# One-hot tables of a graph: wide one-hots and four sums per group, against factored one-hots and one sum

## The reference, cut to what matters

```
attn = ex / denom[src]                                    # softmax over the edges of each src, 4 layers
out = jax.ops.segment_sum(attn[:, :, None] * v[dst], src, num_segments=N)
...
msgs = x[col] * vals[:, None]                             # row = src, col = dst, vals = edge_weight
agg = jax.ops.segment_sum(msgs, row, num_segments=n)
return jnp.einsum('nd,od->no', agg, weight)
```

## Time and profile before

| | |
|---|---|
| time of the kernel, median of 3 runs | 1857.2 us (1856.85 to 1858.12) |
| the profiled execution's own time | 1858.3 us |
| its span in the trace | 1856.5 us |
| loop over the 56 groups, first matmul to last sum | 17.5 to 178.6 us |
| `tables_done` | 179.2 us |

### The profile page before, as it was taken

One profiled execution on the slowest core, in us unless ns is written; L12 is line 12 of the kernel. 1 busy time (PEld: TensorE's weight loads), 2 busy tenths in 40 slices (PEclk: granted clock), 3 DMA queues, 4 the chain that ended last, 5 costly groups with the idle time before them and its releaser, 6 DMA issues.

```text
span 1856.5 us, 30729 instructions
## 1 busy us (share of the span) xinstructions
PE 1746.2 (94%) x11805; PEld 1499.0 (81%) x11805; DVE 1240.5 (67%) x2366; ACT 904.8 (49%) x1468; POOL 432.2 (23%) x545
## 2 busy tenths in 40 slices
PE   4776999999999999999999999999999999999898
PEld 4665788888887888888888888887888888878777
DVE  7888865665866557658665665677557657675744
ACT  9996454554542445446433554554335446453221
POOL 3223230010282301001743010005621001036201
PEclk9898999999999999999999999999999999999899
DMA  3041552242310324224201332332104224240121
GB/s 126 2 131 49 215 174 89 95 129 89 109 44 22 100 78 145 95 75 131 65 26 54 113 122 82 109 115 76 35 30 130 89 80 149 84 152 30 42 88 65
DMA packets 63885, 168.62 MB, mean 91 GB/s; under 512 B 5957, under 2 KB 24250, under 8 KB 63735
## 3 DMA queue, kind: packets, MB, share of 16 engines
q10 hardware_dynamic: 23040, 102.41, 17.1%
q1 hardware_dynamic: 40700, 64.25, 10.8%
HBM read 145.04 MB, written 16.99 MB: 87 GB/s over the span
## 4 chain that ended last, share of the span: by engine, by line
PE 76%; DVE 12%; issue 5%; ACT 3%; DMA 1%; POOL 1%; DVEq 1%; SPq 0%; ACTq 0%; POOLq 0%
PE ps L1501 65%; PE ps L1724 9%; DVE prob L1254 2%; PE ps L1642 2%; DVE onehot L1061 1%; DVE CW L1094 1%; DVE PT_lo L1270 1%; DVE CW L1096 1%; DVE CW L1100 1%; ACT prob L853 1%; POOL x L663 1%; ACT PT_hi L871 1%; DVE CW L1092 1%; DMA piece<-in_L_gnn_m_w_dram 1%; DVEq L1084 1%
## 5 line engine op out<-in xcount | busy, mean ns | idle before, releaser
L871 ACT ACTIVATE PT_hi<-ps 128x512 fp32r<-128x512 f32 (+1 forms) x400 | 235.3, 588 | 244.8 <-PE ps L1724 244.6
L1270 DVE TENSOR_TENSOR PT_lo<-ps,PT_hi 128x512 fp32r<-128x512 f32 (+1 forms) x400 | 270.5, 677 | 50.9 <-ACT PT_hi L871 43.6
L853 ACT ACTIVATE prob<-prob,nmax 128x1250 f32<-128x1250 f32 x160 | 214.2, 1338 | 137.6 <-DVE nmax L1254 137.6
L1724 PE MATMUL ps<-ident,prob 128*128 128x128 f32 (+1 forms) x1600 | 245.3, 276 | 12.5 <-DVE PT_lo L1270 11.9
L1254 DVE CUSTOM_DVE_ANT_0 prob<-ps,Lr 128x1250 f32<-128x1250 f32 x160 | 232.3, 1452 | 32.0 <-PE ps L1501 30.7
L1724 PEld LDWEIGHTS ps<-ident,prob 128*128 128x128 f32 (+1 forms) x1600 | 179.5, 140 | 80.0 <-DVE PT_lo L1270 61.6
L1501 PE MATMUL ps<-PT_hi,v_hi 128*128 128x256 f32 (+1 forms) x800 | 226.7, 283 | 1.2 <-DVE PT_lo L1270 1.2
L1501 PE MATMUL ps<-PT_lo,v_hi 128*128 128x256 f32 (+1 forms) x800 | 225.0, 281 | 0.0
L1501 PE MATMUL ps<-PT_hi,v_lo 128*128 128x256 f32 (+1 forms) x800 | 224.3, 280 | 0.0
L1501 PE MATMUL ps<-yT,wqk_hi 128*128 128x512 f32 (+1 forms) x768 | 213.1, 364 | 0.0
L1501 PE MATMUL ps<-k_hi,q_hi 128*128 128x512 f32 (+2 forms) x480 | 191.9, 400 | 2.1 <-DVE k_lo L1233 2.1
(11 more groups left out here) (210 smaller groups left out, 3801.6 us busy)
## 6 DMA issues: line engine op xcount, KB each, us to landing
Lr<-l_table ACTq DMA_DIRECT2D x160, 625.0 KB, 3.9
piece<-in_L_gnn_m_w_dram SPq DMA_DIRECT2D x32, 256.0 KB, 2.8
w_table<-CW SPq DMA_DIRECT2D x5, 1250.0 KB, 8.0
prob<-w_table SPq DMA_DIRECT2D x10, 625.0 KB, 4.0
x<-in_x_dram SPq DMA_DIRECT2D x2, 2304.0 KB
CW<-CW SPq DMA_DIRECT2D x7, 625.0 KB
piece<-in_L_gnn_wo_dram SPq DMA_DIRECT2D x16, 256.0 KB, 4.8
piece<-in_L_gnn_wq_dram SPq DMA_DIRECT2D x15, 256.0 KB, 2.8
```

What stands on the lines that cost most here:

```text
L853: act.activation(buf, buf, ACT.Exp, bias=nmax[:, i % 4:i % 4 + 1], scale=-1.0, accum_out=prob[:, i % 3, N:N + 1]).then_inc(S["exped"], 1)
L871: act.activation(o, i, ACT.Copy).then_inc(S["pt_hi"], 1)
L1270: dve.tensor_tensor(lo, i, hi.bitcast(F32), ALU.subtract).then_inc(S["pt_split"], 1)
L1724: m = pe.transpose(bank(5 + n % 2, at * P, at * P + rows), prob[0:rows, (NT * h + 2 * g + j) % 3, d * P:(d + 1) * P], ident[0:rows, 0:rows])
```

## The change

A row s is now split into a tile and a rest, s = 128 t + r, and the product is factored the other way round. The left operand is the one-hot of r, 128 columns, as it is and multiplied by the three parts of the weight. The right operand is the one-hot of the place 28 t + (column in the window), 280 columns of fp8.

- VectorE writes the one-hots of r for the three blocks of a group in one compare (`rows`, 3 x 128 places), three groups ahead, behind the sum of the group.
- GpSimd multiplies them by the three parts in one instruction for each group (3 x 3 x 128 = 1152 places).
- ScalarE makes the one-hots of 280 places, three for each group.
- TensorE runs 12 matmuls of 280 columns (3 blocks x 4 parts); the three parts of the weight are summed in PSUM, so VectorE adds counts and weights in one instruction of 560 places.
- Ahead of the loop VectorE works out t, r and the place from the edges; two copies to `eT` that only the fallback needs move behind the first `rows`.
- The other work on VectorE is cut into smaller steps behind groups 4 to 9 (`angles`), 15, 16, 24, 25 (`row_rest`, halves) and 51 to 55 (`early_stats`, one tile each). `cond_rest` and `last_x` on GpSimd stand ahead of groups 36 and 46, and `first_hi` on ScalarE stands behind the loop.
- The loops are written out for all 56 groups, in one branch for each engine but TensorE.

The diff, cut to its core:

```diff
+PLACES = NT * WIN
 ...
-            onehot = sb("onehot", [P, SBUFS, 2, NP], BF16, prep)
-            oh8 = sb("oh8", [P, SBUFS, 2, NP], F8, prep)
+            left = sb("left", [P, SBUFS, GK, 4, P], BF16, prep)
+            right = sb("right", [P, SBUFS, GK, PLACES], F8, prep)
 ...  GpSimd
-            def weigh(c, lo, hi):
-                for part in range(3):
-                    ...
-                    m = pool.tensor_tensor(o, oh, wp.unsqueeze(3).to_broadcast([P, hi - lo, GK, WIN]), ALU.mult)
-                m.then_inc(e_parts, 1)
+            with pool.If(flag < 1):
+                for n in range(NG):
+                    for work in between.get(n, ()):
+                        work()
+                    pool.wait_ge(e_onehot, n + 1)
+                    factors = left[:, n % SBUFS]
+                    pool.tensor_tensor(factors[:, :, 1:4, :], factors[:, :, 0, :].unsqueeze(2).to_broadcast([P, GK, 3, P]),
+                                       wpart[:, :, n, :].rearrange("p k b -> p b k").unsqueeze(3).to_broadcast([P, GK, 3, P]),
+                                       ALU.mult).then_inc(e_parts, 1)
 ...  ScalarE
-                    for b in (2,) if n % CHUNK_G == BOTH else (1, 2):
-                        m = act.activation(oh8[:, n % SBUFS, b - 1, :], iota_h[:], ACT.Abs_reciprocal_sqrt, ...)
+                    for b in range(GK):
+                        m = act.activation(right[:, n % SBUFS, b, :], iota_h[:, 0:PLACES], ACT.Abs_reciprocal_sqrt, ...)
 ...  VectorE, ahead of the loop
+            dve.wait_ge(src_cast, 1)
+            link(dve.tensor_scalar(ef[:, 5, :], ef[:, 0, :], 1.0 / P, -(P - 1.0) / (2 * P), ALU.mult, ALU.add))
+            link(dve.tensor_scalar(ef[:, 5, :], ef[:, 5, :], MAGIC, None, ALU.add))
+            link(dve.tensor_scalar(ef[:, 5, :], ef[:, 5, :], -MAGIC, None, ALU.add))
+            dve.scalar_tensor_tensor(out=ef[:, 4, :], in0=ef[:, 5, :], scalar=-float(P), in1=ef[:, 0, :], ...).then_inc(rows_made, 1)
 ...
+            dve.scalar_tensor_tensor(out=ef[:, 5, :], in0=ef[:, 5, :], scalar=float(WIN), in1=ef[:, 1, :], ...).then_inc(off_made, 1)
 ...  VectorE, the loop
+            def rows(n):
+                dve.tensor_tensor(left[:, n % SBUFS, :, 0, :], iota_h[:, 0:P].unsqueeze(1).to_broadcast([P, GK, P]),
+                                  eT[:, 4, :, n].unsqueeze(2).to_broadcast([P, GK, P]), ALU.is_equal).then_inc(e_onehot, 1)
 ...
+            def group(n):
+                dve.wait_ge(e_sum, START + n + 1)
+                base = dve.value_load(grow_i[0:1, n:n + 1], min_val=0, max_val=N - WIN)
+                sums = ps[:, (n % 2) * 1024:(n % 2) * 1024 + 1024].rearrange("p (k s) -> p k s", k=2)[:, :, 0:PLACES]
+                both = CW[:, :, :, bass.ds(base, WIN)]
+                dve.wait_ge(e_chain, START + n)
+                dve.tensor_tensor(both, both, sums.rearrange("p k (t w) -> p k t w", w=WIN), ALU.add).then_inc(e_chain, 1)
+                if n + AHEAD < NG:
+                    rows(n + AHEAD)
 ...  TensorE
-                    for s in range(NT):
-                        for b in range(GK):
-                            ...
-                            m = mm(ps[:, at:at + 4 * WIN], oh8[...] if by_act else onehot[...], win[...], b == 0, b == GK - 1)
+                    for b in range(GK):
+                        for part in range(4):
+                            o = ps[:, at:at + PLACES] if part == 0 else ps[:, at + 512:at + 512 + PLACES]
+                            m = mm(o, left[:, n % SBUFS, b, part, :], right[:, n % SBUFS, b, :],
+                                   b == 0 and part < 2, b == GK - 1 and part in (0, 3))
```

More of the change, by code:

```diff
@@ L86 @@
 HALF = NP // 2
-BOTH = 0
 HOT = 2.0 ** -6
@@ L107 @@
 )
-assert NT == 10 and NG % UNROLL_G == 0 and UNROLL_G % SBUFS == 0
+assert NT == 10
 LBUFS = 4
@@ L612, in last_x @@
                 pool.memset(x[:, NT - 1, :], 0.0).then_inc(f_set, 1)
[L614 removed]
+            between = {36: (cond_rest,), 46: (last_x,)}
             pool.wait_ge(eplan, 2)
[L617 to L636 removed]
+            flag = pool.value_load(grow_i[0:1, NG:NG + 1], min_val=0, max_val=1)
+            linked = link_n[0]
+            with pool.If(flag < 1):
[7 more added lines that the diff above has]
+                                       ALU.mult).then_inc(e_parts, 1)
+            with pool.Else():
+                link_n[0] = linked
+                for n in sorted(between):
+                    for work in between[n]:
+                        work()
             pool.wait_ge(bias_copied, 1)
@@ L792, in _ @@
                        28: (cond_copy,), 31: (lambda: row_hi(2),), 39: (cond_stack,),
-                       **{44 + 2 * n: (lambda n=n: first_hi(n),) for n in range(AHEAD_PIECES)}}
+                       }
             act.wait_ge(eplan, 2)
@@ L809, in _ @@
                         work()
+            for n in range(AHEAD_PIECES):
+                first_hi(n)
             act.wait_ge(tables_done, 1)
@@ L1051, in _ @@
             dve.wait_ge(iota_cast, 1)
[L1053 to L1068, removed]
+            def rows(n):
+                dve.tensor_tensor(left[:, n % SBUFS, :, 0, :], iota_h[:, 0:P].unsqueeze(1).to_broadcast([P, GK, P]),
+                                  eT[:, 4, :, n].unsqueeze(2).to_broadcast([P, GK, P]), ALU.is_equal).then_inc(e_onehot, 1)
+            for n in range(AHEAD):
+                rows(n)
+            dve.wait_ge(edges_turned, 4)
+            turned(0, 4)
+            turned(2, 5)
             flag = dve.value_load(grow_i[0:1, NG:NG + 1], min_val=0, max_val=1)
@@ L1124, in row_rest @@
-            def row_rest(i):
+            def group(n):
[7 more added lines that the diff above has]
+                    rows(n + AHEAD)
@@ L1133, in _ @@
-            between = {1: (angles,), 2: (lambda: row_rest(0),), 3: (lambda: row_rest(1),), NG // UNROLL_G - 1: (early_stats,)}
-            for i in range(NG // UNROLL_G - 1):
-                for work in between.get(i, ()):
-                    work()
-                with dve.If(flag < 1):
-                    groups(i)
-            for work in between[NG // UNROLL_G - 1]:
-                work()
-            with dve.If(flag < 1):
-                groups(NG // UNROLL_G - 1)
-                dve.wait_ge(e_chain, START + 3 * NG)
-                dve.wait_ge(e_count, START + NG)
+                first_stats(t)
@@ new lines, in _ @@
+            between = {**{4 + n: (lambda n=n: angles(n),) for n in range(6)},
+                       **{15 + 9 * i + n: (lambda i=i, n=n: row_rest(i, n),) for i in range(2) for n in range(2)},
+                       **{NG - EARLY_STATS + t: (lambda t=t: early_stats(t),) for t in range(EARLY_STATS)}}
+            linked = link_n[0]
+            with dve.If(flag < 1):
+                for n in range(NG):
+                    group(n)
+                    for work in between.get(n, ()):
+                        work()
+                dve.wait_ge(e_chain, START + NG)
```

151 lines of the change are left out of this document (58 added, 93 removed).

## The result

The changed kernel takes 1867.5 us against 1857.0 for the kernel before, each the median of six runs: the ratio is 1.0056, with a 95% interval of 1.0044 to 1.0068. One of the six on each side was a slow run (3319 and 7251 us); the medians of the other five are 1866.1 (1864.4 to 1869.1) and 1856.9 (1856.5 to 1858.1). So it is slower, by 9.3 to 10.4 us; the forecast was 1862.5 and slower. The profiled execution took 1864.4 us, 6.1 more than the one shown of before, where the forecast said 5.3 more. It is the shortest of the five; the control and a further trace of this kernel come back to their spread.

A forecast was written before the change was run, and what follows sets the result against it. VectorE set the pace before; GpSimd's product, excluding VectorE's compare, becomes the bound. Start, 56 periods of 2.61, work between groups and tail put `tables_done` at 184.4 against 179.2: 1863.6 profiled, 1862.5 median, range 1832 to 1882.

The forecast's parts named there:

- angles: Angle steps on VectorE between groups: compares and products hold each other off, 7.3 us together, where before it was 6.6.
- `row_rest`: Four halves of this VectorE work between groups: 0.9 us each on the path, 3.7 together.
- the period: Loop, per group: product 2.16, less 0.2 overlap, compare 0.55, 0.1 from compare to product; 2.61 us against 2.48 before.
- The first rival: Loop: compare and product don't exclude one another, so the product alone is the period; 1833 us, chance 0.13.
- the 5 for hidden work: Part of the no-exclusion case: about 5 us of the work between groups would be hidden, besides 25 from the period.
- `make_cond`: Holds TensorE for 6.7 us, its clock low afterwards; with 1.3 to spare in a period, 5.2 us are lost.
- The second and third rivals: GpSimd's product: cheaper, 1.7 us giving 1837 or 1.27 giving 1812 (chance 0.13); or f32 price, 2.70, giving 1892 (0.09).
- The fourth: TensorE falls to its low 1.2 GHz level and bounds the loop: 16 us more, 1879; chance 0.08.
- first product starts: Start: five more VectorE instructions put the plan's end at 15.0 us; the first product follows the first compare at 15.7.
- `cond_rest` and the gap behind it: GpSimd work between groups, in idle time before and now on the path: 2.4 us.
- to `tables_done`: Behind the last product: TensorE 1.8, `base` 0.5, sum 0.74, one tile's statistics 0.9, exit 0.6; 4.55 us.
- The statistics hide, but for the last: VectorE's statistics of tiles cost nothing between groups, except the last tile's 0.9 us behind the last product.

The follow-up runs named there:

- the control: The changed kernel run again with nothing edited, beside the first experiments: 1866.24 us, ratio 1.0060 against the kernel before.
- the version with the product shared: Changed kernel with compare from PSUM, ahead of the wait for the sums, and ScalarE multiplying two of nine blocks: 1830.06 us, ratio 0.9854.
- The kernels with two parts: Third part of the weights left out: of the changed kernel, 1841.98 us; of that with compare from PSUM and ahead of the wait, 1819.05 us.

## Why the prediction was right, point by point

**The bound moved from VectorE to GpSimd, and the period.** Forecast 2.61 us, measured 2.62 in the usual stretch. The product was taken at 2.16 and is 2.13; the gap was taken at 0.45 and is 0.49, since the compare goes on 0.13 us before the traced end of the product and not 0.2. The experiments bear out each half of it: take the exclusion away and the period is the product, shorten the product and the gap stays. The Trainium skill's rule (SBUF — State Buffer, "Who interferes with whom"), that an instruction of VectorE with two inputs from SBUF and one of GpSimd that reads SBUF hold each other off and that with one such input they don't, was the one to trust: 1.57 us with both inputs in SBUF against 0.547 with one in PSUM. The first rival, no exclusion, is thereby refuted for the kernel as it is, and its price was too high where it was brought about: 30 forecast, 22.8 measured. The 25 for the period came (2.62 to 2.10 in 53 periods is 27.6), the 5 for hidden work did not: `hidden_cond` and `make_cond` cost more beside the shorter period, not less. The second and third rivals fall with the 2.13. The fourth doesn't show over the loop: the mean clock from the first to the last product is 0.94, against 0.93 in the earlier trace rows.

**The other terms**, from the first product's start to the signal, in us:

| term | forecast | measured |
|---|---|---|
| first product starts | 15.7 | 16.40 |
| 56 periods, less gaps not there | 145.3 | 146.0 |
| angles | 7.3 | 7.9 |
| `row_rest` | 3.7 | 3.8 |
| `make_cond` | 5.2 | 2.1 |
| `cond_rest` and the gap behind it | 2.4 | 3.15 |
| `last_x` | 0.3 | 0 |
| two products of 2.5 | not foreseen | 0.8 |
| last product ends | 179.9 | 180.13 |
| to `tables_done` | 4.55 | 5.40 |
| `tables_done` | 184.4 | 185.53 |

The periods are 56 products of 2.13 and 55 gaps of 0.49, less 0.2 for the first three products, which stand in a row, and the gap of 1.40 behind them. Each other measured term is a sum over the products or gaps that differ from 2.13 and 0.49: `row_rest` is one of 3.17 and three of 3.04 against four of 2.13, `make_cond` the gap of 2.55 less 0.49. They add up to the last product's end within the rounding.

**The step that failed: `make_cond`.** The forecast let it hold TensorE for 6.7 us, as in the earlier trace rows, and the products behind it for 5.2 (6.7 less the 1.3 to spare is 5.4). Measured are 2.1, for two reasons. The first is the clock. The busy time of one stretch of before, then of two of after (columns as in the earlier trace rows), shows the second half of `make_cond` at the low level before, and all of it at full clock after, with the low level only behind it:

```profile
88.00:92.00 4.00, 4.00 (x21) 4.00 (x20) 2.72 (x3) 4.00 (x4) 0.00 (x0) 0.50 0.00 0
```

```profile
88.00:94.00 6.00, 5.45 (x47) 5.00 (x48) 6.00 (x5) 2.31 (x6) 4.75 (x3) 1.00 0.01 3
94.00:100.00 6.00, 6.00 (x38) 4.36 (x38) 2.48 (x4) 2.73 (x7) 3.22 (x2) 0.72 0.00 0
```

It holds TensorE from 90.1 to 94.66, 4.6 us. The forecast took the duration in one trace as a property of the work, though the clock was part of it. The second reason is a wait that the forecast's own mechanism puts into every period and that it did not take off here. VectorE in order of time:

```profile
92.10 2.05 DVE L1054 TENSOR_TENSOR left<-iota_h,eT 128x384 bf16<-128x384 f16 x1
97.62 0.74 DVE L1080 TENSOR_TENSOR CW<-CW,ps 128x560 f32 x1 [3.47 <-PE ps L1480]
98.27 0.55 DVE L1054 TENSOR_TENSOR left<-iota_h,eT 128x384 bf16<-128x384 f16 x1
```

The sum starts at 97.62, where the pace would have had it at 94.07: 3.55 late. But GpSimd has run out of work by then, so the compare behind it takes 0.55 and not 2.05, and 1.5 of the 3.55 come back. The kernel with the compare from PSUM bears this out: there no compare stands, `make_cond` holds TensorE for 4.8 us at nearly the same clock, and the gap in front of the next product is 5.15:

```profile
93.97 20.70 POOL L619 TENSOR_TENSOR left<-left,wpart 128x1152 bf16<-128x1152 bf16 x9 [5.15 <-DVE left L1055]
```

Three us too much here were made up by small terms that were each too low: the start, the angles, the gap at 131 to 133 us behind `cond_rest`, two products of 2.5 us, and the tail. That the sum came out within 0.8 us of the profiled execution is in this part luck.

**The tail.** "The statistics hide, but for the last" was wrong by 0.85 us. In the last three groups a sum, the statistics of a tile and the read of `base` take VectorE 2.12 us (181.43 to 183.55 between sums), and so it is VectorE that is late at the end, not the way from the last product.

**What cost nothing, as said.** ScalarE's one-hots of 280 places take 0.516 us, not 0.39: the line was laid through 512 places of f32 and 1280 of fp8, and it leads too low here. Three are 1.36 us in a row, still below the period, and TensorE waits for them only 7.5 us in all, 6.9 of it at once. In the version with the product shared this is what fills ScalarE. The sum of 560 places was taken at 0.74 and is 0.730.

**The median.** The profiled execution was forecast at 1863.6 and took 1864.4. For the median the prediction took off 1.1 us, as the kernel before had it; the changed kernel's lies 3.1 above its profiled execution (1.8 by the five runs, 2.1 in the control). That step has no cause behind it that the runs settle.

## What to carry to other kernels

Before work is moved to GpSimd as "idle", ask of every VectorE instruction that will stand beside it where its inputs lie: two engines that exclude one another add up, however much slack each shows by itself. Where an input can stay in PSUM, in which TensorE left it, the same instruction runs beside the product; that one edit turned this change from 0.6% slower to 0.7% faster. A shorter period is not worth its count of groups: check what stands between groups, and whether it was hidden by the slack that goes.

## What the runs showed of the hardware that was not expected

- An exclusion between two in-order engines can have two steady orders, 2.62 and 2.34 us a group with the same instructions, and which one an execution was in went, in three traces, with TensorE's clock in one stretch of 6 us.
- GpSimd's product of bf16 with a repeated weight costs 1.69 ns a place from 768 to 1152 places (1.48 and 2.13 us), close to the slope of the small ones.
- The kernels with two parts lost 4 to 5 us in layers that were the same, with dips of the granted clock in both traces; no run explains them.
